# Two graph layers over one streamed matrix: the blocks that serve both layers are computed as two 64-column halves of the array

## The chip, the cores and the metric

The kernel runs on one core of one Trainium2 chip. The metric is the device time of one launch in microseconds (us). The median of three runs is 977.36 us (977.32 to 977.43). The profile comes from one further execution, which took 975.36 us; its trace covers a span of 973.2 us, and all start times below are counted from the start of that span.

## The reference

The inputs are `x` (8192 x 64), a dense-stored symmetric-pattern matrix `adj` (8192 x 8192, float32, 256 MB) and small parameters. Cut to what matters:

```python
# layer 0
x_drop = x * (u >= 0.1) / 0.9
x = layernorm(x + adj @ x_drop)
# layer 1
x_proj  = tanh(norm(x)) * x / (norm(x) + 1e-8)      # norm of each row, clipped to 10
support = adj @ x_proj
s = clip(norm(support), 0, 0.999)
x = layernorm(x + (arctanh(s) * support / (s + 1e-8)) @ kernel + bias)
```

So `adj` multiplies a 8192 x 64 matrix twice, and the second product needs the normalised result of the first.

## The kernel before, in words

`adj` is cut into 16 x 16 blocks of 512 x 512 values (1 MB each). A block `(r, c)` holds the rows of row block `r` and is stored with its columns on the 128 partitions, as four tiles (`TB = 4`) of 128 x 512. SyncE's queue loads blocks one by one into `ring`, 17 slots of 1 MB (L269), and before a load into a used slot it waits for `block_released`, which TensorE raises at the end of a block.

For one block the stationary operand of a matmul is a piece of `feats`, [128 partitions, 64 features] for each layer, and the moving operand is one tile of the block, 128 x 512. A float32 matmul of the program shows in the trace as two MATMUL instructions, each with its own weight load (LDWEIGHTS). Three kinds of block work exist:

- `first` and `hold` (layer 0 alone) and `part` (layer 1 alone) go through `two_halves` (L511 to L518). It gives tiles t = 0 and 2 to columns 0 to 63 of the array and tiles 1 and 3 to columns 64 to 127. So a block is four matmuls of 64 columns (8 MATMUL rows in the trace), and the two partial sums land in partitions 0 to 63 and 64 to 127 of one PSUM bank. DVE or ACT adds the two later.
- `both` (L526 to L536): the block serves both layers while it is loaded, since the layer 1 features of column block `c < r` are known already. The stationary operand is `feats[:, tile, :, :]`, 128 columns wide (64 of layer 0, 64 of layer 1). A block is four matmuls of 128 columns (8 MATMUL rows). Layer 0 lands in partitions 0 to 63 of `sums_both`, layer 1 in 64 to 127.

`work_order()` (L54) writes the order of all block work by hand. Row block `r` begins with `both` blocks and `first` blocks; after one block stands `turn` of row `r - 1` (the layer norm and the mapping, on DVE, POOL and ACT, which end with `feats` of layer 1 at L418 and the semaphore `mapped`); after five blocks the `part` blocks of column `r - 1` follow, then blocks that are read a second time, then the rest. Over the whole program there are 120 `both` blocks, 136 `first` and `hold` blocks and 136 `part` blocks, 330 loads for 256 different blocks. At the end stand nine `finish` steps (L554 to L567), small matmuls with 64 rows, 128 columns and a moving operand of 128, between runs of `part` blocks.

The array thus changes between two shapes during the main part: 128 x 64 (two halves) and 128 x 128. A run, below, is a stretch of MATMUL instructions of one shape. There are 36 runs of `both`, each with a run of halves before and behind it.

DVE adds each finished partial sum to `support` (L432, L433); TensorE may be four partial sums ahead (`PARTS`, L552).

Of the kernel before, what the change touches and what calls it, by code (L numbers as in the profile page):

```python
# [27 lines left out]
F = 64  # L28
BS = 512
NB = N // BS  # L30
TB = BS // P
# [122 lines left out]
def build(nc, adj, x, u, selector, weight, bias, out):  # L154
# [7 lines left out]
    for _, c, _, _ in loads[:NB]:  # L162
        if c * TB // CHUNK not in chunk_order:
            chunk_order.append(c * TB // CHUNK)
# [8 lines left out]
    def saved_through(r):  # L173

        return 1 + 2 * r

    with ExitStack() as es:
        def sb(name, shape):
            return es.enter_context(nc.sbuf_tensor(name, shape, f32))

        def ps(name):
            return es.enter_context(nc.psum_tensor(name, [P, BS], f32))
# [4 lines left out]
        ring = sb("ring", [P, SLOTS, TB, BS])  # L187
        feats = sb("feats", [P, NT, 2, F])
# [23 lines left out]
        sums_both = [ps(f"sums_both{i}") for i in range(2)]  # L212
# [35 lines left out]
        def half(r):  # L248

            return slice(F * (r % 2), F * (r % 2) + F)  # L250
# [5 lines left out]
        @block.sync  # L256
        def _(sp):
            seen = set()
            for n, (r, c, slot, released) in enumerate(loads):
                chunk = c * TB // CHUNK  # L260
                if r == 0 and n < NB and chunk not in seen:
                    seen.add(chunk)
                    t = slice(chunk * CHUNK, (chunk + 1) * CHUNK)
                    sp.dma_start(xres[:, t, :], x[:, t, :]).then_inc(chunk_loaded[chunk], 16)  # L264
                    sp.dma_start(keep[:, t, :], u[:, t, :]).then_inc(chunk_loaded[chunk], 16)  # L265
                if released:

                    sp.wait_ge(block_released, released)
                sp.dma_start(ring[:, slot], adj[r, c]).then_inc(block_loaded[slot], 16)  # L269
# [89 lines left out]
        def _(dve):  # L359
# [128 lines left out]
            for i, step in enumerate(order):  # L488
                if step[0] == "hold" and step[2] == step[1]:
                    layer1_join(step[1])  # L490
                if step[0] == "turn":
                    layer1_end(step[1])
                if step[0] == "part" and step[5]:
                    _, r, _, n, _, _, _ = step

                    dve.wait_ge(block_released, uses[i][2])
                    add_part(r, n, r == 0 and r not in touched)
                    touched.add(r)
                if step[0] == "finish":
                    square_sums(k)  # L500
                    if k:
                        residual(k - 1)
                    log_scale(k)
                    k += 1
            residual(k - 1)

        @block.tensor
        def _(pe):
            finished = 0

            def two_halves(bank, which, i, start, stop):  # L511

                for t in range(TB):
                    at = F * (t % 2)
                    last = nc.tensor.matmul(bank[at:at + F], feats[:, c * TB + t, which, :],  # L515
                                            ring[:, uses[i][0], t, :],
                                            start=start and t < 2, stop=stop and t >= TB - 2)
                return last  # L518

            for i, step in enumerate(order):  # L520
                kind, r = step[:2]
                if i in uses:
                    c = step[2]
                    slot, nth, _ = uses[i]
                    pe.wait_ge(block_loaded[slot], 16 * nth)
                if kind == "both":  # L526
                    if c == 0 and r >= 2:

                        pe.wait_ge(row_sums_saved, saved_through(r - 2))
                        pe.wait_ge(row_joined, r - 1)  # L530
                    pe.wait_ge(mapped, c + 1)
                    for t in range(TB):
                        last = nc.tensor.matmul(sums_both[r % 2][:], feats[:, c * TB + t, :, :],  # L533
                                                ring[:, slot, t, :],
                                                start=c == 0 and t == 0, stop=c == r - 1 and t == TB - 1)
                    last.then_inc(block_released, 1)  # L536
                if kind in ("first", "hold"):
                    start = c == (r + HELD[r] if r + HELD[r] < NB else NB - 1)
                    if r == 0:
                        pe.wait_ge(dropped, 1 + chunk_order.index(c * TB // CHUNK))  # L540
                    if start and r >= 2:
                        pe.wait_ge(row_joined, r - 1)
                    last = two_halves(sums_first[r % 2], 0, i, start, kind == "hold" and c == r)
                    if kind == "first":
                        last.then_inc(block_released, 1)
                    elif c == r:
                        last.then_inc(row_summed, 1)
                if kind == "part":
                    _, _, _, n, start, stop, _ = step
                    pe.wait_ge(mapped, c + 1)  # L550
                    if start and n >= PARTS:
                        pe.wait_ge(part_added, n - PARTS + 1)  # L552
                    two_halves(sums_part[n % PARTS], 1, i, start, stop).then_inc(block_released, 1)
                if kind == "finish":  # L554
                    rows = r
                    if not finished:
                        pe.wait_ge(params_loaded, 48)
                    pe.wait_ge(part_added, max(last_part[row] for row in rows) + 1)
                    if finished >= 2:
                        pe.wait_ge(projected_read, finished - 1)  # L560
                    for g, row in enumerate(rows):
                        for t in range(TB):
                            last = nc.tensor.matmul(projected[finished % 2][g][:, t, :],  # L563
                                                    support[half(row), row // 2, t * P:(t + 1) * P],
                                                    selw[half(row), :, :], start=True, stop=True)
                    last.then_inc(rows_projected, 1)
                    finished += 1  # L567
# [29 lines left out]
```

## Time and profile before

| what | value |
|---|---|
| median of the runs | 977.36 us |
| profiled execution, its span | 975.36 us, 973.2 us |
| TensorE busy | 921.1 us (95%), 3264 MATMUL instructions |
| DVE busy | 318.5 us (33%) |
| DMA queue that loads `adj` | 350.25 MB, 90.2% of the span |
| mean granted TensorE clock | 0.99 |

"Busy" of TensorE comes from modelled ends of pipelined matmuls, so the starts are the reliable side: the time of a run is read from its first start to the first start of the next run. "PE" is TensorE's matmuls, "PEld" its weight loads, "SPq" the queue that issues the loads of blocks.

### The profile page before, as it was taken

The numbers are of one execution on the slowest core, as the hardware profiler recorded it, in microseconds if no ns is written. First come the engines' busy times: TensorE is split into PE (matmuls) and PEld (weight loads), VectorE is DVE, ScalarE is ACT, GpSimd is POOL, SyncE is SP. The second block draws the span as 40 slices with busy tenths as digits, with TensorE's granted clock in tenths as the row PEclk, the third lists the DMA queues.
The fourth block names the chain that finished last, engine by engine and source line by source line (L and its number), as shares of the span: only waits on it lengthen the run. The fifth ranks groups of instructions, "written<-read, shape, count | busy, mean of one in ns | idle before, by whom it ended". The sixth has DMA issues, their size and how long they took to land.

```text
span 973.2 us, 8646 instructions
## 1 busy us (share of the span) xinstructions
PE 921.1 (95%) x3264; PEld 344.0 (35%) x3264; DVE 318.5 (33%) x1030; ACT 52.5 (5%) x138; POOL 56.9 (6%) x49
## 2 busy tenths in 40 slices
PE   5678999999999999999999999999999999989993
PEld 1122333333333333333333343343433443434441
DVE  1130422315151514332341313303223033076775
ACT  0000000000000000000000000000000000002233
POOL 0000000000000000000000000000000000002332
PEclk9999999999999999999999999999999999999997
DMA  9999999999989999989599895997979989999970
GB/s 369 414 422 421 420 422 421 387 422 373 419 314 422 350 423 376 422 335 389 193 374 422 345 363 198 372 421 260 410 273 368 395 301 398 338 373 421 422 308 32
DMA packets 52599, 352.98 MB, mean 363 GB/s; under 512 B 6224, under 2 KB 8272, under 8 KB 10320
## 3 DMA queue, kind: packets, MB, share of 16 engines
q1 hardware_dynamic: 49824, 350.25, 90.2%
q10 hardware_dynamic: 2736, 2.20, 0.7%
q8 instruction: 26, 0.43, 0.2%
q14 instruction: 13, 0.11, 0.0%
HBM read 350.32 MB, written 2.10 MB: 362 GB/s over the span
## 4 chain that ended last, share of the span: by engine, by line
PE 81%; DMA 12%; SPq 3%; DVE 2%; ACT 1%; issue 1%; POOL 0%; ACTq 0%; POOLq 0%; DVEq 0%
PE sums_both L533 42%; PE sums_part L515 22%; PE sums_first L515 16%; DMA ring<-adj_dram 12%; SPq L269 2%; PE sums_both L563 1%; ACT xres L320 1%; PE sums_first L563 1%; SPq L264 1%; DVE stats L379 0%; POOL rooted L286 0%; DVE y L475 0%; DVE mv L382 0%; SPq L265 0%; DVE feats L475 0%
## 5 line engine op out<-in xcount | busy, mean ns | idle before, releaser
L533 PE MATMUL sums_both<-ring,feats 128*128 128x512 f32 x960 | 421.6, 596 | 2.8 <-DMA ring<-adj_dram 2.8
L515 PE MATMUL sums_first<-ring,feats 128*64 128x512 f32 x1088 | 251.5, 605 | 30.9 <-DMA ring<-adj_dram 30.8
L533 PEld LDWEIGHTS sums_both<-ring,feats 128*128 128x128 f32 x960 | 179.4, 190 | 244.8 <-issue 236.7
L515 PE MATMUL sums_part<-ring,feats 128*64 128x512 f32 x1088 | 240.4, 597 | 3.4 <-issue 3.4
L515 PEld LDWEIGHTS sums_first<-ring,feats 128*64 128x64 f32 x1088 | 73.3, 138 | 204.0 <-issue 139.6
L389 DVE TENSOR_TENSOR row_saved<-sums_both,row_saved 64x512 f32<-64x512 f32 x15 | 10.2, 683 | 390.4 <-ACT row_saved L336 390.4
L515 PEld LDWEIGHTS sums_part<-ring,feats 128*64 128x64 f32 x1088 | 77.7, 137 | 157.8 <-issue 156.8
L432 DVE TENSOR_TENSOR support<-sums_part,support 64x512 f32<-64x512 f32 x94 | 64.3, 684 | 141.3 <-PE sums_part L515 140.9
L296 POOL TENSOR_TENSOR rooted<-base,power 128x8 f32<-128x8 f32 x16 | 27.8, 1736 | 830.5 <-DVE base L405 830.5
L433 DVE TENSOR_TENSOR support<-sums_part,support 64x512 f32<-64x512 f32 x95 | 65.9, 694 | 3.3
L336 ACT COPY row_saved<-sums_first 64x512 f32<-64x512 f32 x16 | 9.3, 580 | 710.5 <-PE sums_first L515 710.5
L400 DVE STREAM_TRANSPOSE turned<-row_saved 32x128 f32<-32x128 f32 x128 | 38.6, 302 | 2.1
L301 POOL TENSOR_TENSOR rooted<-base,power 128x8 f32<-128x8 f32 (+1 forms) x9 | 13.5, 1497 | 61.2 <-DVE base L440 61.2
L373 DVE TENSOR_SCALAR support<-support 128x512 f32<-128x512 f32 x8 | 3.4, 427 | 41.6 <-DMA support<-u_dram 41.6
L379 DVE BATCH_NORM_STATS2 stats<-y 128x6 f32<-128x64 f32 x100 | 14.7, 213 | 0.7
L286 POOL TENSOR_TENSOR rooted<-base,power 128x8 f32<-128x8 f32 (+1 forms) x9 | 13.5, 1498 | 19.7 <-DVE minus_mean L484 19.7
L320 ACT ACTIVATE xres<-y,shift,rooted 128x64 f32<-128x64 f32 x36 | 12.5, 427 | 6.7 <-POOL shift L289 6.7
L440 DVE TENSOR_REDUCE base<-row_saved 128x8 f32<-128x512 f32 (+1 forms) x9 | 5.6, 627 | 21.1 <-ACT row_saved L348 21.1
L382 DVE BATCH_NORM_AGGREGATE mv<-stats 128x2 f32<-128x6 f32 x128 | 11.3, 155 | 0.9
L409 DVE TENSOR_TENSOR below<-rooted 128x4 f32<-128x4 f32 x16 | 2.6, 162 | 25.6 <-POOL rooted L296 25.6
L390 DVE TENSOR_TENSOR row_saved<-sums_first,row_saved 64x512 f32<-64x512 f32 x15 | 10.2, 682 | 0.5
L563 PE MATMUL sums_both<-selw,support 64*128 64x128 f32 x72 | 8.3, 283 | 1.8 <-DVE support L433 1.7
(51 smaller groups left out, 152.9 us busy)
## 6 DMA issues: line engine op xcount, KB each, us to landing
ring<-adj_dram SPq DMA_DIRECT2D x330, 1024.0 KB, 10.2
xres<-x_dram SPq DMA_DIRECT2D x8, 256.0 KB, 15.9
support<-u_dram SPq DMA_DIRECT2D x8, 256.0 KB, 15.8
out_dram<-xres ACTq DMA_DIRECT2D x16, 128.0 KB, 6.0
selw<-selector_dram ACTq DMA_DIRECT2D x1, 32.0 KB, 3.3
selw<-weight_dram ACTq DMA_DIRECT2D x1, 32.0 KB, 3.8
bias_sb<-bias_dram ACTq DMA_DIRECT2D x1, 32.0 KB, 6.3
```

Source lines behind the costliest of these rows:

```text
L269: sp.dma_start(ring[:, slot], adj[r, c]).then_inc(block_loaded[slot], 16)
L286: nc.gpsimd.tensor_tensor(rooted[:, 0, own], base[:, 0, own], power[:, 0, own], ALU.pow).then_inc(deviation_ready, 1)
L296: nc.gpsimd.tensor_tensor(rooted[:, :, 0:TB], base[:, :, 0:TB], power[:, :, 0:TB], ALU.pow).then_inc(root_ready, 1)
L301: nc.gpsimd.tensor_tensor(rooted[:, 1, own], base[:, 1, own], power[:, 1, own], ALU.pow).then_inc(norm_rooted, 1)
L320: last = nc.scalar.activation(xres[:, r * TB + t, :], y_of[k % 2][:, i, :], ACT.Identity, scale=rooted[:, 0, i:i + 1], bias=shift[:, i:i + 1])
L379: last = V.bn_stats(stats[:, t, :], y[:, t, :])
L400: last = V.transpose(turned[q:q + Q, :, f:f + Q], row_tiles[f:f + Q, :, q:q + Q])
L432: done(V.tensor_tensor(total, bank[0:F], total, ALU.add))
L433: V.tensor_tensor(total, bank[F:P], total, ALU.add).then_inc(part_added, 1)
L515: last = nc.tensor.matmul(bank[at:at + F], feats[:, c * TB + t, which, :], ring[:, uses[i][0], t, :], start=start and t < 2, stop=stop and ...
L533: last = nc.tensor.matmul(sums_both[r % 2][:], feats[:, c * TB + t, :, :], ring[:, slot, t, :], start=c == 0 and t == 0, stop=c == r - 1 a ...
L563: last = nc.tensor.matmul(projected[finished % 2][g][:, t, :], support[half(row), row // 2, t * P:(t + 1) * P], selw[half(row), :, :], sta ...
```

## The change

In the `both` step the one matmul of 128 columns for a tile becomes two matmuls of 64 columns over the same moving tile: the layer 0 features go to array columns 0 to 63 and the layer 1 features to columns 64 to 127. The results land where they did, in the same partitions of the same bank. A `both` block is now eight matmuls of the program, 16 MATMUL rows in the trace. Semaphores, waits, the loads, the order of the blocks and the other engines' code are as before. The `finish` matmuls keep their shape.

```diff
@@ -530,9 +530,10 @@
                         pe.wait_ge(row_joined, r - 1)
                     pe.wait_ge(mapped, c + 1)
                     for t in range(TB):
-                        last = nc.tensor.matmul(sums_both[r % 2][:], feats[:, c * TB + t, :, :],
-                                                ring[:, slot, t, :],
-                                                start=c == 0 and t == 0, stop=c == r - 1 and t == TB - 1)
+                        for layer in range(2):
+                            last = nc.tensor.matmul(sums_both[r % 2][layer * F:layer * F + F],
+                                                    feats[:, c * TB + t, layer, :], ring[:, slot, t, :],
+                                                    start=c == 0 and t == 0, stop=c == r - 1 and t == TB - 1)
                     last.then_inc(block_released, 1)
```

TensorE's instructions as the program gives them, in the middle of the program (row block 11: a run of 1 + 4 layer-0 blocks between `both` blocks, then three `part` blocks). A count here is of the program's matmuls; the trace shows two for each.

```order
-L533 MATMUL sums_both<-ring,feats 128x512 x16
+L534 MATMUL sums_both<-ring,feats 64x512 x32
 L515 MATMUL sums_first<-ring,feats 64x512 x4
-L533 MATMUL sums_both<-ring,feats 128x512 x4
+L534 MATMUL sums_both<-ring,feats 64x512 x8
 L515 MATMUL sums_first<-ring,feats 64x512 x20
-L533 MATMUL sums_both<-ring,feats 128x512 x20
+L534 MATMUL sums_both<-ring,feats 64x512 x40
 L515 MATMUL sums_part<-ring,feats 64x512 x12
```

Nothing moved: each `both` matmul has become two of half the width in its place. TensorE at the end of the last row block, where the `finish` steps begin:

```order
-L533 MATMUL sums_both<-ring,feats 128x512 x40
+L534 MATMUL sums_both<-ring,feats 64x512 x80
 L515 MATMUL sums_first<-ring,feats 64x512 x4
 L515 MATMUL sums_part<-ring,feats 64x512 x48
-L563 MATMUL sums_both<-selw,support 128x128 x8
+L564 MATMUL sums_both<-selw,support 128x128 x8
 L515 MATMUL sums_part<-ring,feats 64x512 x20
```

Here too only the `both` rows change; the `finish` rows have a new line number and nothing else. DVE's and SyncE's instructions are the same.

## Rows read from the trace of the kernel before

**Rows 1.** Windows: stretch, busy us (PE, PEld, DVE, ACT, POOL), granted clock, DMA share, GB/s.
```profile
0.00:219.00 219.00, 185.34 (x720) 57.46 (x720) 53.92 (x155) 5.97 (x12) 7.25 (x10) 0.99 1.00 411
219.00:850.00 631.00, 630.97 (x2016) 243.61 (x2016) 179.99 (x464) 15.22 (x35) 19.14 (x11) 1.00 0.91 356
850.00:973.00 123.00, 104.83 (x534) 42.88 (x530) 84.58 (x411) 31.30 (x92) 30.52 (x28) 0.94 0.77 313
```

**Rows 2.** Waits (us, times, longest): TensorE until 219 us, SyncE's queue 219 to 850.
```profile
PE sums_first L515 <- DMA ring<-adj_dram: 30.8, 32, 7.8
...
SPq L269 <- PE sums_both L533: 419.2, 110, 13.7
```

**Rows 3.** Groups by line: busy, mean ns; idle before, releaser.
```profile
L533 PE MATMUL sums_both<-ring,feats 128*128 128x512 f32 x960 | 421.6, 596 | 2.8 <-DMA ring<-adj_dram 2.8
L515 PEld LDWEIGHTS sums_part<-ring,feats 128*64 128x64 f32 x1088 | 77.7, 137 | 157.8 <-issue 156.8
```

**Rows 4.** Timeline of TensorE's matmuls, 490 to 567 us: start, us, run.
```profile
490.20 25.97 PE L515 MATMUL sums_part<-ring,feats 128*64 128x512 f32 x120
516.11 14.00 PE L533 MATMUL sums_both<-ring,feats 128*128 128x512 f32 x32
530.04 1.94 PE L515 MATMUL sums_first<-ring,feats 128*64 128x512 f32 x8
531.90 3.70 PE L533 MATMUL sums_both<-ring,feats 128*128 128x512 f32 x8
535.53 8.80 PE L515 MATMUL sums_first<-ring,feats 128*64 128x512 f32 x40
544.27 17.43 PE L533 MATMUL sums_both<-ring,feats 128*128 128x512 f32 x40
561.63 5.37 PE L515 MATMUL sums_part<-ring,feats 128*64 128x512 f32 x24
```

**Rows 5.** Timeline of TensorE's weight loads, the first ones behind a change of shape.
```profile
530.03 0.20 PEld L515 LDWEIGHTS sums_first<-ring,feats 128*64 128x64 f32 x4 [0.76 <-issue]
```

**Rows 6.** Timeline of TensorE's matmuls, 282 to 303 us: two banks, one shape.
```profile
282.09 10.52 PE L515 MATMUL sums_part<-ring,feats 128*64 128x512 f32 x48
292.44 10.47 PE L515 MATMUL sums_first<-ring,feats 128*64 128x512 f32 x48
302.84 3.70 PE L533 MATMUL sums_both<-ring,feats 128*128 128x512 f32 x8
```

**Rows 7.** Timeline of TensorE's matmuls: first run of L533, runs until 235 us.
```profile
82.84 3.70 PE L533 MATMUL sums_both<-ring,feats 128*128 128x512 f32 x8 [0.57 <-DMA ring<-adj_dram]
...
177.40 10.57 PE L533 MATMUL sums_both<-ring,feats 128*128 128x512 f32 x24 [0.56 <-DMA ring<-adj_dram]
...
219.40 14.00 PE L533 MATMUL sums_both<-ring,feats 128*128 128x512 f32 x32
...
235.09 8.75 PE L515 MATMUL sums_part<-ring,feats 128*64 128x512 f32 x40
```

**Rows 8.** Weight load before the run at 219.40 us, timeline.
```profile
219.40 0.30 PEld L533 LDWEIGHTS sums_both<-ring,feats 128*128 128x128 f32 x2 [0.91 <-DMA ring<-adj_dram]
```

**Rows 9.** Timeline, 812 to 862 us: last run of L533, the turn of row 15.
```profile
812.82 34.60 PE L533 MATMUL sums_both<-ring,feats 128*128 128x512 f32 x80
...
849.11 8.75 PE L515 MATMUL sums_part<-ring,feats 128*64 128x512 f32 x40
...
860.73 0.42 DVE L418 TENSOR_TENSOR feats<-xres,scale 128x256 f32<-128x256 f32 x1
861.26 13.93 PE L515 MATMUL sums_part<-ring,feats 128*64 128x512 f32 x56 [3.39 <-issue]
```

**Rows 10.** Windows in which the loads ran nearly without a pause.
```profile
300.00:400.00 100.00, 100.00 (x349) 36.98 (x346) 36.61 (x90) 2.64 (x6) 3.48 (x2) 1.00 0.98 393
500.00:550.00 50.00, 50.00 (x178) 18.50 (x175) 12.13 (x26) 1.16 (x2) 0.00 (x0) 1.00 0.98 405
```

**Rows 11.** The page's DMA queues: packets, MB, share.
```profile
q8 instruction: 26, 0.43, 0.2%
```

## Prediction

> **What bounds the kernel now.** I read the windows first, since the share of busy time over the whole span mixes stages. They show three stages [rows 1]. Until 219 us the DMA share is 1.00 and TensorE is busy for 185 of 219 us: the loads are the limit. From 219 to 850 us TensorE has no idle time (630.97 of 631.00 us) at a granted clock of 1.00, the 2.4 GHz level, while the DMA engines rest 9% of the time (57 us). From 850 us on come the `finish` steps and a tail. The waits say the same [rows 2]: until 219 us TensorE's layer-0 matmuls wait 30.8 us for loads of blocks. Between 219 and 850 us it is the other way round: no matmul waits for a load, and SyncE's queue waits 419 us for releases by L533 alone. So in the middle stage the loads follow TensorE, and time taken from TensorE there is time taken from the end. What the busy share can't show is whether these 631 us hold anything but streaming. For that I read the timeline of the matmuls, from start to start.
>
> **The price of a change of shape.** Within a run, one MATMUL of 128 columns starts every 0.429 us: the run of 40 lasts 561.63 - 544.27 = 17.36 us, that of 8 lasts 535.53 - 531.90 = 3.63 us, the difference is 13.73 us for 32 [rows 4]. In the halves shape two MATMULs, one on each half, start every 0.429 us: 516.11 - 490.20 = 25.91 us for 120, and 531.90 - 530.04 = 1.86 us for 8, the difference is 24.05 us for 56 pairs. Per column of the array the two shapes thus stream equally fast, and a `both` block costs 8 x 0.429 = 3.43 us in steady state. What is left is paid at the ends of a run. The run of 8 in L533 takes 3.63 - 3.43 = 0.20 us more than its steps, the run of 32 takes 13.93 - 13.73 = 0.20 us more: a change from 128 columns to halves costs 0.20 us. The run of halves of 8 takes 1.86 - 4 x 0.429 = 0.145 us more, that of 120 takes 25.91 - 25.74 = 0.17: a change to 128 columns costs 0.145 us. Its nature shows in the weight loads: at the change out of L533 none is issued for 0.76 us, and the next one, at 530.03 us, starts no earlier than its matmul at 530.04 [rows 4, 5]. The mean MATMUL takes 596 ns against a step of 429 [rows 3], so waiting for the last one to end costs some 0.16 us, about what is seen. It is the shape and not the bank, the line or the semaphore: in 282.09 to 302.84 us `part` blocks are followed by `first` blocks in another bank, and the 20.75 us are 48 steps (20.59) plus one change of 0.16 at the end, with nothing left for the change in the middle [rows 6].
>
> **What the change takes away.** There are 36 runs of L533, from 82.84 us [rows 7] to 812.82 us [rows 9]. Seven of them start before 219 us; the 29 others start with the one at 219.40. Every one of the 29 ends in a change to halves: 29 x 0.20 = 5.8 us. Entries: the one at 219.40 had to wait for its load [rows 8], so it gives nothing, and 28 x 0.145 = 4.1 us. Together 9.9 us.
>
> The seven earlier runs are worth 7 x 0.345 = 2.4 us if all of it came through and 0 if the loads absorb it. The run at 177.40 us still waits for a load, and so does the one at 219.40 [rows 7, 8]; between them TensorE releases slots a little earlier, which can let a load start earlier by one pair of changes. I take 0.3 us, near the lower end, because both runs that border the stretch stood waiting for the loads.
>
> **What it adds.** 960 MATMULs of 128 columns become 1,920 of 64, with as many weight loads. Steps: 120 blocks x 4 tiles x 2 = 960 steps of a pair. The price of one such pair isn't in the trace, since the two now stream the same tile of `ring`, where a pair of L515 streams two different tiles. The nearest row is that of L515: 0.429 us a pair, same widths, same bank for both halves, and the loads of 137 ns (four in 0.86 us) hidden behind the matmuls [rows 3, 4]. I take that, so the block costs 8 x 0.429 = 3.43 us as before: 0. Its bounds: below, I see no gain, because a pair of L515 and a single of L533 have the same step; above, the two could take turns, 960 x 0.429 = 412 us. Both ends are kept for the rivals. More instructions must be fetched too: 8,646 cost 0.43 MB [rows 11], so 1,920 more (MATMUL and LDWEIGHTS, 960 each) are 0.1 MB, at 411 GB/s [rows 1] 0.2 us of DMA time, of which only the part before 219 us can show: 0 to 0.2, I take 0.
>
> **What the gain runs into.** Later than TensorE could come the loads, the mapping, or the end. The loads: with 9% rest in 631 us there are 57 us to spare for 10 us of gain, and since SyncE's queue waits for releases again and again, each load moves forward with TensorE. The mapping: row 15's halves end at about 849.1 us and `feats` is written at 861.15 us, 12.1 us of a chain on ACT, DVE and POOL [rows 9]. The shortest cover for it behind 219 us runs from 219.40 to the first `part` at 235.09 us, 15.7 us [rows 7], and loses one exit, 0.2 us: 3.4 us stay. At the very end of the rows the chain is exposed already (3.39 us idle, between 849.11 and 861.26 us) and has no `both` block in its cover, so it stays and moves as a whole. The `finish` steps from 875 us on use another shape and still change it; nothing there is touched, and what bounds them is released by TensorE, so they move along.
>
> **The sum.** -9.9 - 0.3 + 0 + 0 = -10.2 us. Against the profiled execution: 975.36 - 10.2 = 965.2 us, span 963.0. The runs have a median 2.0 us above the profiled execution (977.36), and I expect the same distance: 967.2 us.
>
> **Rivals.** *The loads take a part back.* In two windows the DMA share is 0.98 [rows 10]; if TensorE can't get ahead there, the changes in them are worth nothing. They hold the starts of nine of the 29 runs (six and three), 9 x 0.345 = 3.1 us, which makes 970.3 us. For it speaks that 2% of 150 us is 3 us of slack, against it that no wait for a load is seen in these windows though the loads are just as dense. Chance 0.10.
>
> *The change doesn't do what it says*: the cost at the ends of a run belongs to something else that changes there, and stays. Then 977.4 us. Rows 6 speak against it, with a change of bank and of operand at no cost; for it only that no change from `both` to `first` within one shape is in the trace. Chance 0.03.
>
> *The halves of one tile get in each other's way, and the kernel is slower.* One mechanism: the two halves can't stream the same tile side by side, and TensorE lets one step end before the next tile begins, as it does at a change of shape, 596 - 429 = 0.167 us at each of the 480 tiles. 40 of these are in the seven early runs (80 MATMULs), 440 x 0.167 = 73 us come through, less 10: about 1040 us. The point from which it decides is low: 10.2 us over 880 steps is 12 ns for a step of 429. Against it: pairs of L515 run without any such loss over 120 MATMULs. Chance 0.05.
>
> *The weight loads come to light.* In L515 a load of 137 ns is fully covered. Were it not in the new pairs, 1,920 x 0.137 = 263 us less the 10 of the gain, of which an eighth lies early: about 1200 us. Chance 0.01. The Trainium skill speaks for this one: "TensorE: Matmul & The Clock Gate", Part 3, the mechanism, says that a weight load overlaps matmuls in flight only where it goes to other row groups of the array, and the two halves share all rows. By that rule L515's 2,176 loads would be exposed already; this trace disagrees, with a step of 0.429 us for a pair [rows 4].
>
> **How the numbers follow.** Forecast 0.81, the loads 0.10, no effect 0.03, the two slower ones 0.06. Less than 0.2% (2 us) is about what a measurement can't tell from no change. Faster by more holds for the forecast and the first rival: 0.91. Within: 0.03. Slower: 0.06. The forecast's own range is 965.0 (the early runs give all of their 2.4 us) to 968.5 (a mis-sized change by a tenth, and the fetches). With the first rival the range is 965.0 to 970.3, which leaves out some 0.1.
>
> **What the profile after would show.** If right: runs of L534 with a start every 0.429 us for two MATMULs and a mean near 596 ns; start to start, a block of 3.43 us and no 0.20 or 0.145 at the ends of runs; weight loads two in each step across the border of a run; the run that starts at 812.82 us now starts about 9.8 us earlier; `finish` steps and tail as long as before; waits for loads only up to about 219 us; a DMA share in the middle stage of 0.92 or 0.93. It would be wrong if the step in L534 is longer than 0.429 us (the pair rivals), if the changes at the borders are still there (no effect), or if waits for loads appear between 300 and 850 us (the loads).

## The result, and the profile after

The changed kernel takes 966.64 us (median of 4 runs, 965.09 to 967.52) where the kernel before takes 977.34 us. The medians differ by 10.7 us. The ratio, taken from all fast runs, is 0.9902, 95% interval 0.9888 to 0.9917: 1.0% or 9.6 us faster (8.1 to 10.9). The forecast median was 967.2 us, 0.6 us more. The profiled execution took 965.09 us, with a span of 963.0 us; 965.2 and 963.0 were forecast.

Windows of the changed kernel (stretch, busy us of PE, PEld, DVE, ACT, POOL, then granted clock, DMA share, GB/s). The middle stage is cut at 840 us, since it is shorter now; they answer to [rows 1]:

```profile
0.00:219.00 219.00, 184.06 (x800) 54.62 (x800) 53.95 (x155) 5.98 (x12) 7.25 (x10) 0.99 1.00 411
219.00:840.00 621.00, 620.91 (x2896) 207.94 (x2896) 180.27 (x465) 15.43 (x35) 19.16 (x11) 1.00 0.92 362
840.00:963.00 123.00, 104.62 (x532) 42.77 (x528) 84.38 (x411) 31.09 (x92) 30.54 (x28) 0.94 0.77 313
```

The first stage and the last have kept their length; the middle one has lost 10 us, and TensorE is as full in it as before. Weight loads take less of it, though twice as many are made for a `both` block (137 ns for 64 columns, two at a time, in place of 190 ns for 128 columns): they are hidden either way.

The timeline of TensorE's matmuls in the changed kernel, the runs that answer to [rows 4]:

```profile
485.28 25.92 PE L515 MATMUL sums_part<-ring,feats 128*64 128x512 f32 x120
511.03 13.90 PE L534 MATMUL sums_both<-ring,feats 128*64 128x512 f32 x64
524.76 1.89 PE L515 MATMUL sums_first<-ring,feats 128*64 128x512 f32 x8
526.48 3.60 PE L534 MATMUL sums_both<-ring,feats 128*64 128x512 f32 x16
529.91 8.75 PE L515 MATMUL sums_first<-ring,feats 128*64 128x512 f32 x40
538.50 17.34 PE L534 MATMUL sums_both<-ring,feats 128*64 128x512 f32 x80
555.66 5.32 PE L515 MATMUL sums_part<-ring,feats 128*64 128x512 f32 x24
```

Read it from start to start. A run of one `both` block lasts 529.91 - 526.48 = 3.43 us, which is 8 steps of 0.429 and nothing more; before it was 3.63 us. A run of one `first` block lasts 1.72 us, before it was 1.86. The whole piece from the start of the 120 `part` MATMULs to the start of the next 24 `part` MATMULs lasts 70.38 us; before, 71.43 us. That is 1.05 us for three round trips, 0.35 us each.

The weight loads of the changed kernel at the border at 511.03 us show why; they answer to [rows 5]:

```profile
510.17 0.14 PEld L515 LDWEIGHTS sums_part<-ring,feats 128*64 128x64 f32 x2 [0.28 <-issue]
510.60 0.14 PEld L534 LDWEIGHTS sums_both<-ring,feats 128*64 128x64 f32 x2 [0.29 <-issue]
511.03 0.14 PEld L534 LDWEIGHTS sums_both<-ring,feats 128*64 128x64 f32 x2 [0.29 <-issue]
```

Two loads every 0.43 us go across the border, and the first ones of L534 are made at 510.60 us, one step ahead of their matmul at 511.03. The 0.76 us without a load have gone.

The first and last run of the middle stage and the tail, from the same timeline; they answer to [rows 7, 9]:

```profile
219.15 13.95 PE L534 MATMUL sums_both<-ring,feats 128*64 128x512 f32 x64
...
802.86 34.50 PE L534 MATMUL sums_both<-ring,feats 128*64 128x512 f32 x160
837.20 1.89 PE L515 MATMUL sums_first<-ring,feats 128*64 128x512 f32 x8
...
851.05 13.93 PE L515 MATMUL sums_part<-ring,feats 128*64 128x512 f32 x56 [3.38 <-issue]
864.91 2.05 PE L564 MATMUL sums_both<-selw,support 64*128 64x128 f32 x16
...
948.82 1.16 PE L564 MATMUL sums_both<-selw,support 64*128 64x128 f32 x8 [1.69 <-DVE support L433]
```

The run that began at 219.40 us now begins at 219.15, the one at 812.82 at 802.86. The pause behind row 15 is what it was (3.38 us against 3.39). Who waited for whom in the changed kernel, TensorE over the whole span (total us, times, longest); the answer to [rows 2]:

```profile
PE sums_first L515 <- DMA ring<-adj_dram: 31.9, 32, 7.6
PE sums_part L515 <- issue: 3.4, 1, 3.4
PE sums_both L534 <- DMA ring<-adj_dram: 2.7, 5, 0.6
PE sums_both L564 <- DVE support L433: 1.7, 1, 1.7
```

The waits for loads have not grown by more than about 1 us, and by the same view none of the matmuls' waits lies between 219 and 850 us. Only the weight load ahead of the run at 219.15 us still waits for its block, 1.0 us against 0.9 before.

To compare kernels below I use two stretches of the matmul timeline besides the times. The *rows* stretch runs from the start of the first `both` run behind 219 us to the start of the halves behind the last `both` run. The *end* stretch runs from there to the start of the last `finish` run. The load-limited stage ahead of both differs by some us between executions of one kernel, and they leave it out.

| kernel | rows, us | end, us |
|---|---|---|
| before | 627.95 | 111.67 |
| changed | 837.20 - 219.15 = 618.05 | 948.82 - 837.20 = 111.62 |
| changed, second profile | 618.05 | 111.45 |
| halves in the last block only | 624.86 | 112.72 |
| halves in all but the last block | 621.79 | 111.66 |
| halves in two tiles of four | 656.32 | 109.96 |
| changed, finish in halves | 618.05 | 109.30 |
| layer loop outside | 633.44 | 111.97 |
| late column | 618.05 | 109.91 |
| late column, finish in halves | 618.05 | 109.47 |
| pause filled | 618.05 | 109.86 |
| pause filled, finish in halves | 618.05 | 109.25 |

In the column *end*, differences of 1 us and more come from TensorE's granted clock behind a pause, and not from the shape of the `both` blocks; this is taken up with the finish matmuls below.

The kernel before ran at 974 to 979 us beside the experiments, with a median of 976.4 to 976.7 us.

### The profile page after: what moved, and what is told of

It is laid out like the page before. It is cut to its first block, busy times and chain, and to the rows that moved or that the text cites. A ratio compares the mean times of both kernels' runs of the same rounds, so it can differ in the third digit from the quotient of the medians.

```text
span 963.0 us, 10566 instructions
## 1 busy us (share of the span) xinstructions
PE 909.6 (94%) x4224; PEld 305.3 (32%) x4224; DVE 318.6 (33%) x1030; ACT 52.5 (5%) x138; POOL 57.0 (6%) x49
## 4 chain that ended last, share of the span: by engine, by line
PE 79%; DMA 13%; SPq 3%; DVE 2%; ACT 1%; issue 1%; POOL 0%; ACTq 0%; POOLq 0%; DVEq 0%
PE sums_both L534 41%; PE sums_part L515 22%; PE sums_first L515 15%; DMA ring<-adj_dram 13%; SPq L269 2%; PE sums_both L564 1%; ACT xres L320 1%; PE sums_first L564 1%; SPq L264 1%; DVE stats L379 0%; POOL rooted L286 0%; DVE y L475 0%; SPq L265 0%; DVE mv L382 0%; DVE feats L475 0%
## 5 line engine op out<-in xcount | busy, mean ns | idle before, releaser
L534 PE MATMUL sums_both<-ring,feats 128*64 128x512 f32 x1920 | 418.4, 592 | 2.8 <-DMA ring<-adj_dram 2.7
L515 PE MATMUL sums_first<-ring,feats 128*64 128x512 f32 x1088 | 250.2, 603 | 32.2 <-DMA ring<-adj_dram 31.9
L515 PE MATMUL sums_part<-ring,feats 128*64 128x512 f32 x1088 | 239.9, 596 | 3.4 <-issue 3.4
L534 PEld LDWEIGHTS sums_both<-ring,feats 128*64 128x64 f32 x1920 | 137.4, 137 | 278.8 <-issue 270.7
L515 PEld LDWEIGHTS sums_first<-ring,feats 128*64 128x64 f32 x1088 | 75.8, 138 | 200.4 <-issue 133.5
L515 PEld LDWEIGHTS sums_part<-ring,feats 128*64 128x64 f32 x1088 | 78.6, 138 | 155.8 <-issue 154.9
L341 ACT ACTIVATE tanh<-norm 128x4 f32<-128x4 f32 x16 | 3.3, 205 | 125.3 <-DVE norm L410 125.3
```

Source lines behind the costliest of these rows:

```text
L534: last = nc.tensor.matmul(sums_both[r % 2][layer * F:layer * F + F], feats[:, c * TB + t, layer, :], ring[:, slot, t, :], start=c == 0 and ...
```

## The experiments

### Halves in the last block only, and in all but the last

The first question is whether the price stands at the borders or in the blocks. Two complementary kernels of before and after:

```diff
                     for t in range(TB):
-                        for layer in range(2):
-                            last = nc.tensor.matmul(... 64 columns ...)
+                        if c == r - 1:        # the second kernel: c < r - 1
+                            for layer in range(2):
+                                last = nc.tensor.matmul(... 64 columns ...)
+                        else:
+                            last = nc.tensor.matmul(... 128 columns ...)
```

> The changed kernel, but with halves only in the last both block of each row block (c == r - 1, 15 of the 120 blocks, mostly runs of one block between layer-0 blocks); the other 105 stay at 128 columns. Theory (a fixed price at each border between the two shapes): of the 57 changes of shape behind 219 us 39 are left, 18 go, 9 x 0.345 = 3.1 us, with some 0.2 us from the early part 3.3: about 974.0 us. Rival (a block in halves is itself cheaper, whatever stands beside it): 15/120 of the 10.7 us, 1.3 us: about 976.0 us.

> The complement: halves in the 105 both blocks with c < r - 1, 128 columns in the 15 blocks with c == r - 1. Theory (price at the borders): 22 changes of shape are left behind 219 us, 35 go, 17 x 0.145 + 18 x 0.20 = 6.1 us, with 0.2 early 6.3: about 971.0 us. Rival (cheaper blocks): 105/120 of 10.7 us, 9.4 us: about 968.0 us.

Halves in the last block only: 972.60 us, ratio to the kernel before 0.9955 (0.9940 to 0.9969), so 3.0 to 5.9 us less; 1.3 us, the rival's figure, lies outside. All but the last block: 970.02 us, ratio 0.9934 (0.9922 to 0.9946), 5.3 to 7.6 us less; the rival's 9.4 us lies outside too. Both medians are lower than expected, by 1.4 and 1.0 us; executions of one kernel differ by more than that (970.5 to 974.2 us for the first). The traces are sharper. From 220.22 to 845.08 us and from 220.06 to 841.85 us the rows stretches are 624.86 and 621.79 us, 3.09 and 6.16 us less than before; 3.1 and 6.1 were expected. 15 converted blocks brought half as much as 105. The timelines, first of the last block only, then of all but the last:

```profile
530.88 3.60 PE L535 MATMUL sums_both<-ring,feats 128*64 128x512 f32 x16
534.32 8.75 PE L515 MATMUL sums_first<-ring,feats 128*64 128x512 f32 x40
543.00 17.43 PE L539 MATMUL sums_both<-ring,feats 128*128 128x512 f32 x40
560.36 5.37 PE L515 MATMUL sums_part<-ring,feats 128*64 128x512 f32 x24
```

```profile
529.19 3.70 PE L539 MATMUL sums_both<-ring,feats 128*128 128x512 f32 x8
532.82 8.80 PE L515 MATMUL sums_first<-ring,feats 128*64 128x512 f32 x40
541.46 17.34 PE L535 MATMUL sums_both<-ring,feats 128*64 128x512 f32 x80
558.62 5.32 PE L515 MATMUL sums_part<-ring,feats 128*64 128x512 f32 x24
```

In the first kernel the single block in halves takes 534.32 - 530.88 = 3.44 us and the five blocks at 128 columns 17.36; in the second the single block of 128 columns takes 3.63 us and the five in halves 17.16. Each run of `both` is 0.20 us longer when it is of the other shape than what follows, whether it holds one block or five.

The run of 40 `first` MATMULs between the two tells more. It is 20 steps, 8.58 us, in both. In the first kernel only what follows it is of the other shape, and it lasts 543.00 - 534.32 = 8.68 us: the change to 128 columns costs 0.10 us. In the second only what stands ahead of it is, and it lasts 541.46 - 532.82 = 8.64 us: 0.06 us of the change out of 128 columns fall behind the border. So a change out of 128 columns costs about 0.25 us and one into it 0.10. The prediction had 0.20 and 0.145, because every run of halves that it measured had both kinds of border. The round trip, 0.345 us, is the same.

### The shape changed inside every block

```diff
                     for t in range(TB):
-                        for layer in range(2):
-                            last = nc.tensor.matmul(... 64 columns ...)
+                        if t < 2:
+                            for layer in range(2):
+                                last = nc.tensor.matmul(... 64 columns ...)
+                        else:
+                            last = nc.tensor.matmul(... 128 columns ...)
```

> Tiles 0 and 1 of each both block in halves, tiles 2 and 3 at 128 columns, so the shape changes inside every block. Theory (price at the borders): 219 changes behind 219 us in place of 57, 109 x 0.145 + 110 x 0.20 = 37.8 us against 9.9, so 27.9 us more than the kernel before: about 1005 us, every tile pair with a border of 0.20 or 0.15 us. Rival (cheaper tiles in halves): half of the gain, 972 us.

1005.73 us, ratio 1.0295 (1.0278 to 1.0312). The rows stretch is 656.32 us, 28.4 us more than before, with 27.9 expected. (The expectation counts 219 changes; each of the 110 blocks has one in and one out, 220, which makes it 28.1.) Its timeline:

```profile
530.68 1.94 PE L535 MATMUL sums_both<-ring,feats 128*64 128x512 f32 x8
532.54 1.98 PE L539 MATMUL sums_both<-ring,feats 128*128 128x512 f32 x4
534.46 1.94 PE L535 MATMUL sums_both<-ring,feats 128*64 128x512 f32 x8
```

Either piece is four steps, 1.72 us; in halves that is 8 MATMULs, at 128 columns 4. It takes 534.46 - 532.54 = 1.92 us at 128 columns and 532.54 - 530.68 = 1.86 us in halves: 0.20 and 0.14 at the ends, in the middle of a block, with no semaphore, bank or line of the order changed there. So the shape alone carries the price.

### The loops exchanged

```diff
-                    for t in range(TB):
-                        for layer in range(2):
+                    for layer in range(2):
+                        for t in range(TB):
```

> The changed kernel with the loops of a both block exchanged: the four tiles of layer 0 one after the other on columns 0 to 63, then the four of layer 1 on columns 64 to 127. The same 1,920 MATMULs, one shape. Theory: two halves run side by side only when neighbours in the queue are on different halves (two MATMULs of a tile on one half, two on the other); eight in a row on one half take a step of 0.43 us each, so a block takes up to 6.9 us in place of 3.43, 110 blocks behind 219 us: up to 377 us more, about 1340 us. Rival: TensorE looks ahead far enough to pair them all the same: 967 us.

984.09 us (two executions, 981.84 and 986.35), ratio 1.0079 (1.0048 to 1.0111): 17 us more than the changed kernel, not 377. The theory fell; the rival was right that the halves still run side by side, and wrong that it is free. The timeline of TensorE's matmuls behind 534 us:

```profile
534.57 0.64 PE L515 MATMUL sums_first<-ring,feats 128*64 128x512 f32 x1
534.99 0.59 PE L534 MATMUL sums_both<-ring,feats 128*64 128x512 f32 x1
535.05 0.59 PE L515 MATMUL sums_first<-ring,feats 128*64 128x512 f32 x1
```

L515's matmuls come after all those of L534 in the program, yet the first starts at 534.57 us while L534's go on. The halves thus each follow their own order, and one may be some steps ahead of the other. What it costs is seen in the weight loads of the same kernel:

```profile
530.10 0.19 PEld L534 LDWEIGHTS sums_both<-ring,feats 128*64 128x64 f32 x2 [0.24 <-issue]
530.59 0.14 PEld L534 LDWEIGHTS sums_both<-ring,feats 128*64 128x64 f32 x1 [0.29 <-issue]
531.01 0.19 PEld L534 LDWEIGHTS sums_both<-ring,feats 128*64 128x64 f32 x3 [0.29 <-issue]
...
532.36 0.14 PEld L534 LDWEIGHTS sums_both<-ring,feats 128*64 128x64 f32 x1 [0.29 <-issue]
```

From 530.10 to 530.59 us is a step of 0.49, to 531.01 one of 0.42, and three more make 1.35 us (0.43, 0.43 and 0.49). So one step in four is long by 0.06 us. If all blocks are like this one, that is 2 x 0.06 us a block, 110 blocks, an estimate of 13 of the 15.4 us that the rows stretch has grown by (633.44 against 618.05). Where the other 2 us and that 0.06 come from was not tried.

### The finish matmuls in halves

```diff
                         for t in range(TB):
-                            last = nc.tensor.matmul(projected[finished % 2][g][:, t, :],
-                                                    support[half(row), row // 2, t * P:(t + 1) * P],
-                                                    selw[half(row), :, :], start=True, stop=True)
+                            for at in range(0, P, F):
+                                last = nc.tensor.matmul(projected[finished % 2][g][at:at + F, t, :],
+                                                        support[half(row), row // 2, t * P + at:t * P + at + F],
+                                                        selw[half(row), :, :], start=True, stop=True)
```

> The changed kernel, and the finish matmuls too in two 64-column halves (64 rows stay). There are nine finish runs, each with an entry that cost 0.16 us and an exit of some 0.2. Theory A (only the number of columns is the shape): nine round trips go, 9 x 0.35 = 3.1 us, about 963.5 us, less if DVE holds the last ones. Theory B (the number of rows is part of the shape): 128 x 64 to 64 x 64 costs as before, 966.6 us, within 0.5.

963.88 us, ratio 0.9869 (0.9856 to 0.9883), an interval that lies below that of the changed kernel. By the time alone theory A, which gave 963.5 us, would win; the trace says otherwise. Runs of the matmul timeline, first of the changed kernel's second profile, then of this one:

```profile
870.07 8.80 PE L515 MATMUL sums_part<-ring,feats 128*64 128x512 f32 x40
878.80 1.71 PE L564 MATMUL sums_first<-selw,support 64*128 64x128 f32 x16
880.44 8.80 PE L515 MATMUL sums_part<-ring,feats 128*64 128x512 f32 x40
```

```profile
851.65 12.24 PE L515 MATMUL sums_part<-ring,feats 128*64 128x512 f32 x56 [3.38 <-issue]
863.82 1.96 PE L565 MATMUL sums_both<-selw,support 64*64 64x128 f32 x32
865.71 8.80 PE L515 MATMUL sums_part<-ring,feats 128*64 128x512 f32 x40
874.45 1.59 PE L565 MATMUL sums_first<-selw,support 64*64 64x128 f32 x32
875.97 8.80 PE L515 MATMUL sums_part<-ring,feats 128*64 128x512 f32 x40
```

The 40 MATMULs of halves ahead of a finish run last 8.73 us in the one and 8.74 us in the other, 20 steps and 0.15: the changes are paid as before, and theory A is wrong. Theory B, that the rows of the shape count as well as its columns, fits. It is not isolated: a finish matmul also has a moving operand of 128 in place of 512, and no kernel here changes that length or the rows alone. Another operand, another bank and a semaphore are no cause: with the pause filled (below), 40 MATMULs stand ahead of added ones in halves that differ in these three, and they last 848.28 - 839.69 = 8.59 us, 20 steps and nothing more. Only the finish runs got 0.1 us shorter, 0.6 us from the first to the last. The rest of what the time showed is elsewhere: the seven `part` blocks behind the pause took 863.82 - 851.65 = 12.17 us here and 864.91 - 851.05 = 13.86 us in the changed kernel. One row of the windows for 840 to 870 us explains it, first of the changed kernel's second profile, then of this kernel (the last three figures are granted clock, DMA share, GB/s); the third row is 3 us of the changed kernel's first profile, right behind the start at 851.05 us:

```profile
840.00:870.00 30.00, 26.62 (x124) 10.01 (x120) 20.36 (x48) 1.27 (x3) 1.74 (x1) 0.94 0.96 379
```

```profile
840.00:870.00 30.00, 26.62 (x148) 10.45 (x146) 21.91 (x55) 3.00 (x7) 3.38 (x2) 1.00 0.98 390
```

```profile
852.00:855.00 3.00, 3.00 (x10) 1.10 (x8) 1.78 (x4) 0.00 (x0) 0.00 (x0) 0.50 1.04 415
```

TensorE stood still for 3.38 us in all three. In the changed kernel its granted clock then was at the 1.2 GHz level for a while (0.50 from 852 to 855 us), in this kernel it stayed at 2.4 GHz. The finish matmuls stand behind this stretch, so nothing here says why. The finish runs (0.6 us) and the clock (1.7 us, if it stayed up in the other executions too, which no trace shows) make 2.3 of the 2.8 us between the medians; the rest is open.

### The changed kernel again, and the pause moved

```diff
-    order += reread(COLUMN_AFTER - TURN_AFTER, last) + column(last)
+    order += reread(COLUMN_AFTER - TURN_AFTER + 2, last) + column(last)
```

> The changed kernel once more, on the same chip as the two kernels built upon it: 0.990 of the kernel before, about 966.9 us against 977.3. In the profiled execution before, TensorE's granted clock fell in the pause behind row 15 (0.91 in 840 to 860 us) and steps took 0.86 us in place of 0.43 for a while, 1.7 us in all; in the one with the finish halves it did not (1.00). If that is a matter of the moment, executions of this kernel differ by up to 1.7 us.

> The changed kernel with two more blocks that are read again ahead of the part blocks of column 15, so that TensorE has 7 instead of 5 blocks of halves (12.0 us) over the 12.1 us that row 15's chain of mapping takes. Theory: the pause of 3.4 us goes, the clock stays at 1.00, and 3.4 to 5.1 us are gained against the changed kernel: 962 to 963.5 us. Rival: the same pause comes back as a wait of the last finish steps for DVE's additions, since the two blocks are missing at the end (the last run of part blocks has 16 MATMULs, not 32): 966.9 us.

> The kernel with the late column and the finish matmuls in halves of 64 columns. From the trace of the finish halves: 83.28 us from the first finish run to the last in place of 83.91, so 0.6 us less than the late column alone: 961.5 to 963 us. If the shape's rows didn't count, the nine entries of 0.16 us would be gone as well, 1.4 us more.

The changed kernel: 966.78 us, ratio 0.9905 (0.9889 to 0.9922), as before. Its rows stretch is again 618.05 us, while the `both` run behind 219 us began at 222.48 us instead of 219.15. Its clock fell again (0.91 in 840 to 860 us), so these two profiles do not differ in it.

The late column: 966.43 us, ratio 0.9897 (0.9878 to 0.9915), no difference from the changed kernel that can be measured. The rival was right. Its timeline at the end:

```profile
841.01 24.36 PE L515 MATMUL sums_part<-ring,feats 128*64 128x512 f32 x112
...
940.43 3.65 PE L515 MATMUL sums_part<-ring,feats 128*64 128x512 f32 x16
949.20 2.07 PE L564 MATMUL sums_both<-selw,support 64*128 64x128 f32 x8 [5.12 <-DVE support L433]
```

The pause behind row 15 is gone, and the wait of the last finish run for DVE is 5.12 us in place of 1.69: the 3.4 us have moved there. The end stretch is 109.91 us, 1.7 less than 111.62, which is the clock that no longer falls (1.00 in 840 to 860 us). With the finish in halves as well: 965.27 us where 961.5 to 963 were expected, ratio 0.9884 (0.9868 to 0.9900), end stretch 109.47 us. So the theory's gain of 3.4 us didn't come in either kernel, and a 1.7 us gain of the trace is too small for the times to show.

### The pause filled

```diff
                     _, _, _, n, start, stop, _ = step
+                    if c == NB - 1 and not filled:
+                        filled = True
+                        pe.wait_ge(row_sums_saved, saved_through(NB - 2))
+                        pe.wait_ge(row_joined, NB - 1)
+                        for _ in range(6):
+                            at = F * (_ % 2)
+                            nc.tensor.matmul(sums_both[0][at:at + F], feats[:, 2 * CHUNK, 0, :],
+                                             feats[:, 2 * CHUNK:2 * CHUNK + TB, :, :], start=True, stop=True)
                     pe.wait_ge(mapped, c + 1)
```

The second kernel has the finish matmuls in halves besides, by the diff shown above.

> The changed kernel, and ahead of the part blocks of column 15 six added matmuls whose result nobody reads (12 MATMUL instructions of halves in a bank that is free, 2.6 us) inside the pause of 3.4 us. Theory (the granted clock falls because TensorE stands still behind row 15): the pause shrinks to about 0.8 us of standing still, the clock stays at 1.00 and the seven part blocks behind it take 12.2 us in place of 13.8: 1.6 us less from 219 us on than the changed kernel (729.6 us from the first both run behind 219 us to the last finish run), 728.0; about 965.3 us. Rival (the steps there are slow for another reason, such as DVE's additions coming late): 729.6, no change, 966.8 us.

> The same added matmuls, and the finish matmuls in halves of 64 columns. The trace of the finish halves, whose clock had stayed up, had 727.35 us for the same stretch; with the clock kept up in every execution the same 727.4, 0.6 us less than the added matmuls alone: about 964.7 us, 0.987 of the kernel before, the fastest of all. It would be wrong if the stretch is 729 us again.

963.77 us, ratio 0.9869 (0.9850 to 0.9889), and 963.61 us, ratio 0.9873 (0.9849 to 0.9898). The timeline of the first:

```profile
848.28 2.75 PE L558 MATMUL sums_both<-feats 128*64 128x512 f32 x12
851.78 12.24 PE L516 MATMUL sums_part<-ring,feats 128*64 128x512 f32 x56 [0.76 <-DVE feats L418]
863.95 2.05 PE L573 MATMUL sums_both<-selw,support 64*128 64x128 f32 x16
```

TensorE stands still for 0.76 us, and the seven blocks take 863.95 - 851.78 = 12.17 us. Rows and end together are 727.91 us (728.0 expected) and 727.30 us (727.4 expected), against 729.67 us of the changed kernel. The times are 1.5 and 1.1 us below the expected ones. These two and the finish halves alone (963.88 us) are the shortest of all and can't be told apart by the times. The intervals of these two touch or overlap that of the changed kernel, so the traces show that they are faster than it, and the times don't.

With the pause as it was the clock stayed up in two profiles of eight. If that were chance here too, both profiles with the pause filled would show it once in 16 times, and these two and the two of the late column together once in 256 (estimates from two of eight).

## Why the prediction was right

- **What bounds.** The middle stage was TensorE's, from start to start, and the changed kernel's DMA share of 0.92 there was within what was named.
- **The price of a change of shape.** The round trip of 0.345 us, read from runs of two lengths, held to the hundredth: 57 changes were to give 9.9 us, and the rows stretch went from 627.95 to 618.05, 9.90 us. The partial kernels and the mixed one scale with the number of borders (3.09 and 6.16 us saved for 3.1 and 6.1, 28.4 us added for 27.9). How it is shared between the two directions was read wrongly, 0.20 and 0.145 in place of about 0.25 and 0.10. Rows 6 already show it: the first run there is 24 steps and 0.05 us, the second 24 steps and 0.10, so the "0.16 at the end" is the rest of an earlier change out of 128 columns and one change in. The sum didn't suffer, since out and in come in pairs.
- **The total.** That the profiled execution came within 0.1 us is luck: executions of the changed kernel range from 965.09 to 968.34 us, and the profiled one was the shortest. The median lay 1.6 us above it and not 2.0. The last `both` run was to start 9.8 us earlier and started 9.96 earlier; the prediction's own prices give 28 x 0.345 + 0.3 = 9.96.
- **Entry at 219.40 us and the early runs.** 0.3 us was taken for all that lies ahead; the profiles show 219.15 against 219.40, 0.25 us. That is luck as much as reading, since the same kernel began that run at 222.48 us in its second profile. No run here isolates the early part.
- **The added pairs.** The one price without a row, two halves that stream the same tile, was taken from L515 at 0.429 us and is 0.429 us. The rival with 0.167 us a tile is dead with it. That pairs needn't even stand next to each other in the queue came out only in the experiment with the loops exchanged.
- **The weight loads.** They stayed hidden, 4,096 of 64 columns at 137 ns, at two a step. The Trainium skill's sentence ("TensorE: Matmul & The Clock Gate", Part 3, The mechanism) that they overlap only with other row groups does not hold for two column halves in these traces. The same section also allows a load into the background weight buffer; no run here shows which buffer a load uses.
- **The loads, the mapping, the end.** No matmul's wait for a load appeared between 219 and 850 us, the cover of the mapping sufficed, and the end stretch moved as a whole (111.67 and 111.62 us). What I had not seen is that this end stretch contains 1.7 us of a lowered clock, in both kernels: I had read the pause of 3.39 us and not the steps behind it. It did no harm to the sum because it was in both.
- **Its nature.** I named a wait for the last matmul's end, 0.16 us. The two directions cost 0.25 and 0.10 us, and neither is that figure. That the price is a wait for the array to run empty fits the weight loads that stop for 0.76 us, and the Trainium skill ("TensorEngine Tiling (Array Packing)", Key Properties) says that a change of tiling mode drains TensorE. What was shown is that the change of shape costs it; that it is a drain was only argued. The modelled ends don't settle it: by them the run of 32 ends at 516.11 + 14.00 = 530.11 us, 0.07 us behind the start of the next [rows 4].

## What to carry to other kernels

When TensorE has no idle time, measure its runs from start to start at two lengths: what doesn't grow with the length is paid at the borders, and here it was 0.35 us for each trip to another array shape and back. To divide it between the two directions, look at runs that have the other shape on one side only. A float32 product of 128 columns cost nothing more here as two 64-column halves that take turns in the queue (1,920 against 960 MATMULs, 0.429 us a step), so a kernel that mixes both widths can keep one. Going to 64 rows, with a shorter moving operand, still cost 0.15 us. And behind every pause of TensorE look at the granted clock of the steps that follow.

## What had not been expected

- Behind a pause of 3.4 us the granted clock fell to the 1.2 GHz level in some executions and not in others: a step took 0.86 us in place of 0.43 for four or so steps. The seven blocks behind the pause took 13.7 to 13.9 us in five profiles and 15.0 in that of halves in the last block only, where they take 12.17 at the full clock: 1.5 to 2.8 us lost. It fell in these six profiles, those of both kernels among them, and stayed up in two, that of the finish halves and that of the mixed blocks; with a pause of 0.76 us it stayed up in both profiles. That it fell because TensorE stood still is what the filled pause supports; why it falls in some executions only is open.
- Two column halves of the array run in their own order: with four tiles of one half ahead of four of the other in the program, they still overlapped, for 0.14 us more a block (15.4 us over 110 blocks).
- The load-limited first stage of one and the same kernel ended 3.3 us later in another execution (222.48 against 219.15 us), more than the 3.1 us that the halves in the last block save. Stretches of the trace told 0.1 us apart where the times didn't tell 1.7.
